# A routed mixture-of-experts block on one core: zero rows written at the front of each expert's region, and POOL's products done one iteration earlier

## What is computed

```python
mod = (silu(c) @ wmod).reshape(1, 6, 1, 512)          # sa, ca, ga, sb, cb, gb
ga, gb = (sign(g) * maximum(abs(g), 0.25) for g in (ga, gb))
h = layernorm(x) * (1 + ca) + sa
x = x + ga * (tanh(h @ B.T) @ C.T + D * h)            # D: one factor per column
h = layernorm(x) * (1 + cb) + sb
scores = sigmoid(h @ gate_w.T)                        # 8 experts
idx = top_k(scores + router_bias, 2)                  # two experts per token
w = scores at idx, divided by their sum
y = sum over the two experts e of w_e * ((silu(h @ W1[e]) * (h @ W3[e])) @ W2[e])
shared = (silu(h @ sw1.T) * (h @ sw3.T)) @ sw2.T      # 704 hidden columns
x = x + gb * (y + shared)
```

## Time and profile before

| what | value |
|---|---|
| median of 3 runs (lowest, highest) | 610.11 us (609.97, 612.59) |
| the profiled execution | 610.75 us |
| its span, first to last instruction | 609.1 us |
| busy: PE, PEld | 565.2 us (93%), 508.9 us (84%) |
| busy: DVE, POOL, ACT | 321.6 us (53%), 242.4 us (40%), 178.1 us (29%) |
| mean granted clock of TensorE | 0.981 |
| chain that ended last, by engine | PE 67%, issue 12%, DVE 9%, POOL 5%, DMA 4%, ACT 2% |
| HBM read, written | 71.73 MB, 30.67 MB |

### The profile page before, as it was taken

The page is one execution under the profiler, slowest core; times in us unless marked ns, Lnnn a source line. Parts: engine busy times, 40 slices in busy tenths (PEclk is TensorE's granted clock), DMA queues, the critical chain, the costliest instruction groups (busy, mean ns, idle before and its releaser), DMA issues.

```text
span 609.1 us, 11649 instructions
## 1 busy us (share of the span) xinstructions
PE 565.2 (93%) x3304; PEld 508.9 (84%) x3305; DVE 321.6 (53%) x642; ACT 178.1 (29%) x332; POOL 242.4 (40%) x201
## 2 busy tenths in 40 slices
PE   4986899999999885999989999989999999999995
PEld 2655888988988774899979999979999998999994
DVE  3599788878876874432222222222222226666766
ACT  1344243344344131232222322223222322121220
POOL 1698674674683361340073500266160003322231
PEclk9998899999999988899999999999999999999999
DMA  8985193222222226952268632567662234554443
GB/s 312 369 278 207 52 346 123 87 103 97 75 104 104 102 91 223 345 209 96 85 216 317 230 121 80 161 216 268 239 224 71 69 101 143 163 170 151 141 140 116
DMA packets 37576, 102.72 MB, mean 169 GB/s; under 512 B 4272, under 2 KB 4272, under 8 KB 36656
## 3 DMA queue, kind: packets, MB, share of 16 engines
q1 hardware_dynamic: 27968, 53.65, 25.4%
q0 software_dynamic: 9152, 47.98, 22.1%
q10 hardware_dynamic: 432, 0.79, 0.3%
HBM read 71.73 MB, written 30.67 MB: 168 GB/s over the span
## 4 chain that ended last, share of the span: by engine, by line
PE 67%; issue 12%; DVE 9%; POOL 5%; DMA 4%; ACT 2%; SPq 1%; DVEq 0%; POOLq 0%; ACTq 0%
PE bank L808 11%; PE bank L810 11%; PE bank L809 11%; PE bank L822 6%; PE bank L824 6%; PE bank L823 6%; PE bank L794 4%; PE bank L829 3%; PE bank L899 2%; POOL wlo L474 2%; PE bank L764 2%; PE bank L763 2%; PE bank L765 2%; DMA whi<-w_all 2%; DVE sel L1087 1%
## 5 line engine op out<-in xcount | busy, mean ns | idle before, releaser
L808 PE MATMUL bank<-whi,thi 128*128 x416 | 140.2, 337 | 4.6 <-POOL wlo L474 4.6
L810 PE MATMUL bank<-whi,tlo 128*128 x416 | 135.2, 325 | 0.0
L809 PE MATMUL bank<-wlo,thi 128*128 x416 | 135.1, 325 | 0.0
L822 PE MATMUL bank<-whi,gth 128*128 (+1 forms) x204 | 81.6, 400 | 3.2 <-DVE gtl L1064 1.6
L808 PEld LDWEIGHTS bank<-whi,thi 128*128 128x128 f32 x416 | 79.1, 190 | 5.8 <-issue 5.8
L474 POOL TENSOR_TENSOR wlo<-raw,whi 128x1408 f32 (+3 forms) x21 | 69.0, 3308 | 35.4 <-DMA whi<-w_all 35.3
L1434 DVE TENSOR_TENSOR gbuf<-s,bank 128x352 f32<-128x352 f32 x52 | 27.0, 519 | 103.7 <-ACT s L742 103.4
L1438 DVE TENSOR_TENSOR gtl<-bank,gth 128x384 fp32r<-128x384 f32 x52 | 29.0, 558 | 97.8 <-ACT gth L746 97.8
L824 PE MATMUL bank<-whi,gtl 128*128 (+1 forms) x204 | 80.5, 395 | 0.0
L823 PE MATMUL bank<-wlo,gth 128*128 (+1 forms) x204 | 80.5, 395 | 0.0
L809 PEld LDWEIGHTS bank<-wlo,thi 128*128 128x128 f32 x416 | 79.3, 191 | 0.0
(11 more groups left out here) (180 smaller groups left out, 1046.0 us busy)
## 6 DMA issues: line engine op xcount, KB each, us to landing
raw<-w_all POOLq DMA_DIRECT2D x7, 2176.0 KB, 9.2
whi<-w_all POOLq DMA_DIRECT2D x14, 704.0 KB, 10.0
h<-xs_rows SPq DMA_DIRECT2D x36, 256.0 KB, 2.8
ys_rows<-tmpa SPq DMA_DIRECT2D x36, 256.0 KB, 2.1
x_all<-wmod SPq DMA_DIRECT2D x6, 1024.0 KB, 8.4
whi<-w_all POOLq DMA_DIRECT2D x7, 768.0 KB, 13.1
hs_rows<-h SPq DMA_DIRECT2D x8, 512.0 KB, 2.8
h<-hs_rows SPq DMA_DIRECT2D x16, 256.0 KB, 2.7
```

Of the source, the lines that this page charges most:

```text
L808: pe.matmul(dst, xh[:, j, a], wh, start=(m == 0), stop=False)
L809: pe.matmul(dst, xh[:, j, a], wl, start=False, stop=False)
L810: mm = pe.matmul(dst, xl[:, j, a], wh, start=False, stop=(m == KD - 1))
L822: pe.matmul(dst, gth[:, a], wh, start=(m == 0), stop=False)
```

## The change

Four things, by the diff.

- The zero rows of an expert stand ahead of its rows and not behind. The offsets start at `e * R + 128`, and the table gives the first tile of an expert the row `e * R + 128 + n - 128 * tiles` (`lead` holds the difference). The rows `e * R` to `e * R + 127` of all experts are zeroed by one DMA of 2 MB that SP issues early, ahead of its wait for the last modulation. `pad`, its semaphores and the copy of the counts go.
- VectorE's `table_rows` has four more small instructions on the way to `s_row` (`lead` twice, `rmt`, `tr`) and `routed` one more.
- POOL's `times_d` and `with_d` for pair `it` are done in iteration `it`, behind the square roots and ahead of `fetch` and the scatter, from iteration 3 on. Those of pair 2 stay ahead of iteration 3.
- In the last iteration TensorE's `last_tile` stands behind `up`, right ahead of `ranks`, and not ahead of the gate matmuls.

```diff
@@ -283,13 +282,6 @@
         def live(lag, lo, hi):
             return lo - lag >= 0 and hi - lag < NP
-
-        def pad(eng, first, end, done):
-
-            eng.wait_ge(s_cnt, 1)
-            for e in range(first, end):
-                n = eng.value_load(ti[0:1, TB_N + e:TB_N + e + 1], min_val=0, max_val=T)
-                eng.dma_start(xs[bass.ds(n + e * R, P), :], zrow[:, :]).then_inc(done, 16)
 
@@ -353,6 +345,8 @@
                          zrow[:, :].unsqueeze(1).to_broadcast([P, SMAX - SMIN, D])).then_inc(s_pad, 16)
             sp.dma_start(xs[E * R:, :], zrow[:, :]).then_inc(s_pad, 16)
+            sp.dma_start(xs[0:E * R, :].rearrange("(e r) d -> r e d", r=R)[0:P],
+                         zrow[:, :].unsqueeze(1).to_broadcast([P, E, D])).then_inc(s_pad, 16)
             sp.wait_ge(s_mod, 6)
@@ -381,9 +375,7 @@
                 sp.dma_start(xin[:, j, :], src[bass.ds(row, P), :]).then_inc(q["S", "xin"][j], 16)
 
-            pad(sp, 0, E - PAD_ACT, s_pad)
-            sp.wait_ge(s_pad, 16 * (E - PAD_ACT + 2))
-            sp.wait_ge(s_pad_act, 16 * PAD_ACT)
+            sp.wait_ge(s_pad, 48)
             sp.wait_ge(s_scat, 64 * NP)
@@ -480,21 +472,15 @@
                     pool.tensor_tensor(tmpa[:, j, :], tbuf[:, j, :], a12[:, 0, :], ALU.mult).then_inc(s_xa, 1)
 
-            def with_d(it, lo, hi):
-                if live(1, lo, hi):
-                    p = it - 1
-                    if lo > 2:
-                        times_d(p)
-                    pool.wait_ge(s_xa, p * 2 + 2)
-                    for j in range(2):
-                        pool.tensor_tensor(tmpa[:, j, :], tmpa[:, j, :], a12[:, 1, :], ALU.add).then_inc(s_xb, 1)
-                    pool.wait_ge(s_xb, p * 2 + 2)
-                    xp = x_all[:, bass.ds(p * 2, 2), :]
-                    pool.tensor_tensor(xp, xp, tmpa[:, :, :], ALU.add).then_inc(s_xd, 1)
+            def with_d(p):
+                pool.wait_ge(s_xa, p * 2 + 2)
+                for j in range(2):
+                    pool.tensor_tensor(tmpa[:, j, :], tmpa[:, j, :], a12[:, 1, :], ALU.add).then_inc(s_xb, 1)
+                pool.wait_ge(s_xb, p * 2 + 2)
+                xp = x_all[:, bass.ds(p * 2, 2), :]
+                pool.tensor_tensor(xp, xp, tmpa[:, :, :], ALU.add).then_inc(s_xd, 1)
 
             def body(it, lo, hi):
-                if lo > 2:
-                    with_d(it, lo, hi)
                 if lo == 2:
@@ -513,7 +499,10 @@
                     pool.tensor_tensor(rs1[:, :], ve1[:, :], mhalf[:, :], ALU.pow).then_inc(s_rs1, 1)
                 if lo == 2:
-                    with_d(it, lo, hi)
+                    with_d(1)
+                if lo > 2 and live(0, lo, hi):
+                    times_d(it)
+                    with_d(it)
 
@@ -572,6 +561,8 @@
             pool.tensor_tensor(down_a, down_a, mods[:, 5, :].unsqueeze(1).to_broadcast([P, KF, D]),
                                ALU.mult).then_inc(s_w2g, 1)
+            times_d(2)
+            with_d(2)
             iterations(pool, body, 3)
@@ -685,8 +676,6 @@
                 if live(1, lo, hi):
                     states(it - 1, lo)
-                if is_last(lo):
-                    pad(act, E - PAD_ACT, E, s_pad_act)
                 if live(3, lo, hi):
@@ -884,8 +873,6 @@
                     down("A", it - 4, 1, 0, 0)
 
-                if is_last(lo):
-                    last_tile()
                 if live(3, lo, hi):
@@ -921,6 +908,7 @@
 
                 if is_last(lo):
+                    last_tile()
                     ranks()
@@ -1143,18 +1131,19 @@
             def table_rows():
                 dve.wait_ge(s_rt, NP * KR)
-                link(dve.tensor_tensor(nE[:, :], rbase[:, :], const("eoff"), ALU.subtract))
+                link(dve.scalar_tensor_tensor(nE[:, :], rbase[:, :], -float(P), const("eoff"), ALU.add, ALU.subtract))
                 b3 = big3[:, 0:E * NT].rearrange("p (e t) -> p e t", e=E)
                 link(dve.tensor_tensor(b3, nE[:, :].unsqueeze(2).to_broadcast([P, E, NT]),
                                        const("thr").unsqueeze(1).to_broadcast([P, E, NT]), ALU.is_gt), False)
-                dve.tensor_copy(ti[:, TB_N:TB_N + E], nE[r0, :]).then_inc(s_cnt, 1)
                 dve.wait_ge(chain, count[0])
                 link(dve.tensor_reduce(tl[:, :], b3, AX.X, ALU.add))
                 link(dve.tensor_scalar(ne[:, :], tl0, 1.0, None, ALU.min), False)
                 link(dve.tensor_tensor_scan(cum[:, :], const("ones")[:, 0:E], tl[:, :], 0.0, ALU.mult, ALU.add), False)
-                link(dve.tensor_scalar(rmt[:, :], tl0, -float(P), float(R), ALU.mult, ALU.add))
-
-                link(dve.tensor_copy(ne[:, 0:1], one[:, 0:1]), False)
+                link(dve.tensor_scalar(lead[:, 0:E], tl[:, :], -float(P), float(P), ALU.mult, ALU.add), False)
+                link(dve.tensor_scalar(rmt[:, :], nE[r0, :], -1.0, float(R - P), ALU.mult, ALU.add))
+                link(dve.tensor_tensor(lead[:, 0:E], lead[:, 0:E], nE[:, :], ALU.add), False)
+                link(dve.tensor_copy(ne[:, 0:1], one[:, 0:1]))
+                link(dve.tensor_tensor(rmt[:, :], rmt[:, :], lead[r0, 1:E + 1], ALU.add), False)
                 link(dve.tensor_tensor(ge, per(steps_c, S), over(cum, S), ALU.is_ge))
@@ -1162,6 +1151,7 @@
                 link(dve.tensor_reduce(tq[:, 0:S], nums, AX.X, ALU.add), False)
                 link(dve.tensor_copy(tq[:, S:S + 1], last_n))
+                link(dve.tensor_scalar(tr[:, :], tr[:, :], lead[r0, 0:1], None, ALU.add))
                 dve.scalar_tensor_tensor(ti[:, TB_ROW:TB_ROW + S], steps_c, float(P), tr[:, :],
@@ -1328,7 +1318,8 @@
 
             body(0, 0, 0)
-            link(dve.tensor_copy(rbase[:, :], const("eoff")))
+            link(dve.tensor_scalar(rbase[:, :], const("eoff"), float(P), None, ALU.add), False)
+            link(dve.memset(lead[:, E:E + 1], 0.0))
             link(dve.tensor_copy(ti[:, TB_PAR:TB_PAR + E + 4], const("par")[0:1, :]))
@@ -1377,6 +1368,7 @@
                 link(dve.scalar_tensor_tensor(base[:, :], base[:, :], float(P), const("eoff"),
                                               ALU.mult, ALU.subtract))
+                link(dve.tensor_tensor(base[:, :], base[:, :], lead[:, 0:E], ALU.subtract))
                 for k in range(2):
```

More of the change, by code:

```diff
@@ L47 @@
 R = T + P
-PAD_ACT = 3
 KR, KM, KB = 12, 6, 9
@@ L68 @@
 TB_FIN = TB_ORDER + E + 2
-TB_N = TB_FIN + E + 2
-TB_ITERS = TB_N + E
+TB_ITERS = TB_FIN + E + 2
 TB_JEND = TB_ITERS + 1
@@ L160, in build @@
         rmt = sb("rmt", [1, E])
+        lead = sb("lead", [P, E + 1])
         ordn = sb("ordn", [1, E])
@@ L237, in build @@
         s_rank = sem("s_rank")
-        s_cnt, s_row, s_tab = sem("s_cnt"), sem("s_row"), sem("s_tab")
-        s_pad, s_pad_act = sem("s_pad"), sem("s_pad_act")
+        s_row, s_tab = sem("s_row"), sem("s_tab")
+        s_pad = sem("s_pad")
         w_hi, w_raw, w_ready = [sem(f"w_hi{k}") for k in range(NW)], sem("w_raw"), sem("w_ready")
```

## The result

The changed kernel took 609.12 us (median of 20 runs, 606.84 to 611.02), the kernel before 610.50 us (20 runs, 609.27 to 613.11) on the same chip. The ratio is 0.9972, with a 95% interval from 0.9963 to 0.9982: some 0.3% faster, where 0.4% was forecast. The profiled execution took 608.43 us, with a span of 606.8 us and a mean granted clock of 0.983.

What follows compares the result with a forecast made beforehand. TensorE is busy almost throughout; the largest hole precedes the expert part. -4.56 + 1.7 - 0.8 + 1.3 = -2.4 us from 610.75 gave 608.4 profiled, 607.7 us median; range 605.3 to 611.3, the forecast's own 606.5 to 609.0.

Steps and rivals of the forecast that it cites:

- rival C: Last iteration and transition: two clock falls, or a scatter landing slowly even without zero writes; 609.7 us, chance 0.20.
- A: Last iteration: the clock holds, so moving `last_tile` loses only 0.2 us; 606.5 us, chance 0.20.
- B: Iteration 3: VectorE keeps its turn, so `first_weights` is not held by POOL; 606.4 us, chance 0.13.
- Part 1: Transition to the expert part: without late zero writes, the first load of sorted rows goes out 4.56 us earlier.
- Part 2: Last iteration: `last_tile` behind `up` costs 0.2 us by order and 1.5 by one clock fall; 1.7 lost, bounds 0.2 and 3.2.
- Part 3: Behind the transition: the shorter hole leaves a shorter low-clock stretch; 0.8 us gained, bounds 0 and 1.6.
- Part 4: POOL's products in their own iteration: steady iterations lose 0, iteration 3 loses 1.3 us once; bounds 0 and 2.7.
- POOL takes its turn between the two: Iteration 3: waiting POOL goes between VectorE's `slo` and `first_weights(2)`, delaying TensorE's `down`; 1.3 us lost, once.
- The queue in iteration 4: Expert weights issued 7.5 us later delay the scatter's landing to 100.2; `idx` at 101.5 leaves 1.3 us margin, no cost.
- the forecast's own list: Signs of being wrong: iteration 0.3 us longer, iteration 4's `idx` awaiting DMA, scatter landing over 3 us, iteration 3's `down` on time.
- D: Steady iterations and iteration 3: POOL gets its turn ahead of `slo`; 613.1 us, chance 0.08, or 0.12 with iteration 3's queue overrunning.
- The reading that was weighed there: Last iteration: gate matmuls count as work, the hole alone is too short; loss 0.2 us, whole sum 1.5 better.

Runs made afterwards that it cites:

- the hole filled: Changed kernel, `last_tile` still behind `up`, with 9 same-sized matmuls of unused result ahead of the last iteration's gate matmuls: 605.23 us, ratio 0.9928.
- the low parts early: Changed kernel, `last_tile` in its old place, POOL's second-weight low parts of iterations 8 and 9 ahead of the scatter: 604.41 us, again 604.67 us.

## Why the prediction was right, step by step

The time fell within 1.4 us of the forecast, and three of the four terms had the right cause and sign; the fourth, POOL's, did not occur. But the sizes were off, and the errors cancelled. The measured 609.12 us lies just outside the forecast's own 606.5 to 609.0, and nearer to rival C's 609.7 than to 607.7. The lower bound of the whole range, 605.3, is not the sum of what it names: A and B together give 605.2, and either one with 0.8 more from the clock 605.6 or 605.7; the upper, 611.3, comes to 611.0 by its own terms (609.7, and half of 2.7). Nothing hangs on it here.

- *Part 1, the zero rows: 4.56 forecast, 4.28 measured*, 4.24 with the tile in place. The landing and the first load took 2.79 us, and not 1.85 + 0.74 = 2.59. The table of rows, written at 233.58, was hidden as said: the landing ended at 233.46 + 2.73 = 236.19.
- *Part 2, the tile behind `up`: 1.7 forecast, 4.15 measured.* This is the term that was mis-sized. Its 0.2 for the order was right: with the hole filled, `ranks` start 222.15 - 211.11 = 11.04 us into the iteration, and 10.83 in the kernel before (223.13 - 212.30). The fall of the clock came too, as in the earlier trace rows, and the experiment with the hole filled shows that it is the rest of the cost. But the step "I take one such fall", of 3.4 us behind the gate and with it "the gate's first matmuls slower", was too small: the clock had fallen in the hole already (0.76 as its mean), ahead of the narrow matmuls and not behind them, so that the gate took 3.58 us and not 1.95, 1.6 more, and it stayed low for 8.8 us, so that `up`, from 218.3 to 224.7, took 6.4 us and not the 3.90 of the earlier trace rows, 2.5 more. The mask came at 222.09, 10.56 us into the iteration, as before; `up` and the tile, which had ended with it, now ended 4.1 later. Even the upper bound, 3.2, was too low. The working also took the clock of today's last iteration as full: behind the wait for the mask, right after the row 221.40:224.10 of the earlier trace rows, it was at 0.55, and the move took that away. The gain lay off the path to the load, so the sum did not need it.
- *Part 3, the clock behind the transition: 0.8 forecast, 1.38 measured*, inside its bounds in the changed kernel. In the kernel with front zero rows alone it was 1.9, over the bound of 1.6: with the load another 4.1 us earlier the low stretch goes altogether.
- *Part 4, `first_weights(2)` held: 1.3 forecast, 0 measured.* The step "POOL takes its turn between the two" failed: VectorE, with its next instruction ready, kept its turn, and POOL's first multiply waited for two VectorE instructions. It is what rival B said. Steady iterations: `slo` goes first, as said, `ra` was held (0.84 to 1.17 us long in iterations 4 to 7, where 0.3 to 0.6 was forecast) and `idx` too, which was not foreseen; both are covered, and an iteration is 22.52 us. The queue in iteration 4 cost nothing, but its margin was not 1.3 us: SP's load of h rows, which waits for the same landing, was issued at 100.00 (100.2 forecast), and `idx` came at 100.03 and not at 101.5; it was held by POOL (2.01 us in all). With the tile in its old place, where both should be the same, `idx` came at 100.31 after 0.42 us of waiting for the DMA. By the forecast's own list that was a sign of being wrong; it too cost nothing, with iterations of 22.53 us.
- Not foreseen: an iteration is 0.09 us shorter, and iteration 4 starts 0.32 earlier; together the 0.77 us at the start of the last iteration. The 0.32 proves nothing: iteration 4 starts between 76.81 and 79.42 in the profiled executions of all kernels here. The 0.09 is more than that: all kernels with front zero rows have 22.52 to 22.54 in the steady iterations, all with the old zero rows 22.61 or 22.62, whatever stands on POOL. In iteration 7 the first product of `up` has a mean of 330 ns before and 326 after, the other two 323 and 324, and 322 and 323. Why is open; no run tells it apart.

Of the rivals, A (the clock holds) fell: to hold it took work in the hole. B was right in its mechanism and had the loss of part 2 wrong, as the forecast did. C named what happened, more low clock than one fall's, and its load 1.3 us or less earlier was 0.13; but it kept the 1.3 of part 4, and had 0.4 where part 3 gave 1.38. D (POOL ahead of `slo`) did not happen.

The profiled executions differ by -4.28 + 4.15 - 1.38 + 0 - 0.77 = -2.3; the forecast was -4.56 + 1.7 - 0.8 + 1.3 = -2.4. That they are so near is luck. The medians differ by 1.4 only, as the profiled execution of after is one of its faster ones (608.43, against a median of 609.12).

The reading that was weighed there (the Trainium skill, TensorE: Matmul & The Clock Gate, Part 1 and "Why this matters for your kernels"), by which this hole is too short to matter, is not what the trace shows: a hole of 2.15 us was followed by 8.8 us of TensorE's work at 0.50.

The best of what was run is the kernel before with front zero rows alone: 604.4 and 604.0 us, 1.0% under the kernel before and 0.7 to 0.8% under the changed one. The changed kernel with the low parts early and the tile in place (604.4, 604.7) is equal to it, with more in it.

## What to carry to other kernels

Ask of each matmul that you move not only where it lands, but what it leaves behind: 9 matmuls that took a place where TensorE would otherwise wait held the clock, and without them 2.15 us of nothing cost 4.15. When you price a fall of the clock, count all the work that stands in the low stretch, and check whether what is "hidden in a wait" is still hidden once everything in front of it takes twice as long. The same 9 matmuls show the other side too: moved into the wait for the mask they kept the clock up there, and the kernel with both waits filled has no fall at either place. And split a change of several parts before judging it: with the tile in its old place it gave 0.7%, and an edit that nothing else in the change needed left 0.3%.

## What the runs showed of the hardware

- The 16 gate matmuls, 8 columns wide, take 1.95 us at full clock and 3.58 us at 0.50. Behind the hole of 2.15 us the clock stayed at 0.50 through 8.8 us in which TensorE was busy without a gap. In the kernel before, the hole of 5.12 us was followed by a low clock until 248.2; in the kernel with front zero rows two holes around 235 to 237.6, with 0.87 and 1.06 us before the transposes, left it at 1.00. That is no rule: in the kernel with the tile in its old place two such holes, of 0.79 and 1.02 us, were followed by 0.50 in 238 to 240. Behind the wait for the mask, 1.66 us in the kernel before and 1.72 with front zero rows alone, the clock fell both times.
- Which of VectorE and POOL goes first when both want to start is not one rule in these traces. POOL's multiply went ahead of `slo` at 31.78 in the kernel before and at 31.44 in the changed one, and waited for `wlo` at 71.31 after the change. In both cases the one that had been waiting was POOL. What decides is open. Once POOL's long instruction has begun, the other side is held for all of it: 3.7 us for a `sel` that takes 0.18.
- SP's first load came 7.15 us after the end of the last scatter instruction with the eight late zero writes, and 2.79 us without them. With them the DMA engines were full (386 GB/s from 234 to 236), and the chain of waits runs over the last zero write; when the scatter itself had landed does not show.
